# The last tile's second half in two quarters of 256 columns, with a third store at the end

## What is computed

```python
out = conv1d(x, weight, padding=4, groups=4)             # (64, 64, 1024)
y = out + (cond @ c_weight.T)[:, :, None] + bias[None, :, None]
base = y @ kernel + ffn_bias                             # 1024 x 1024
A_eff, B_eff = gate mixed lora_A, lora_B                 # rank 32, one for each of 8 blocks of sequences
delta = (y @ A_eff.T) @ B_eff.T + (y @ A_shared.T) @ B_shared.T
result = x + base + delta
```

## Time and profile before

| | |
|---|---|
| median of 3 runs | 509.15 us (508.51 to 509.65) |
| profiled execution | 507.94 us |
| its span | 506.1 us |
| PE busy | 488.4 us, 96% |
| weight loads (PEld) | 403.1 us, 80% |
| DVE, POOL, ACT busy | 332.9, 272.7, 166.7 us |
| last of PE's products ends | 500.91 us |
| DMA | 65.04 MB, mean 129 GB/s |

### The profile page before, as it was taken

How to read it: one execution, slowest core, us unless ns; L and a number is a source line. 1 busy time by engine, 2 the same in 40 slices (tenths; PEclk the granted TensorE clock), 3 DMA queues, 4 the chain that set the end, 5 groups by cost and what they waited for, 6 DMA issues and landing times.

```text
span 506.1 us, 6740 instructions
## 1 busy us (share of the span) xinstructions
PE 488.4 (96%) x2394; PEld 403.1 (80%) x2394; DVE 332.9 (66%) x384; ACT 166.7 (33%) x210; POOL 272.7 (54%) x157
## 2 busy tenths in 40 slices
PE   2999998999999999999999999999999999999995
PEld 2777886788888888888888888888888888888884
DVE  4786585996938497575939397575948488473411
ACT  2566313341525123331524224331433234331100
POOL 0789943792847439272756529282665619382200
PEclk9999999899999999999999999999999999999998
DMA  8953526751724326241634326241633313241303
GB/s 216 416 217 138 188 69 172 243 199 67 240 94 114 83 70 239 51 128 41 230 102 111 86 52 241 57 124 55 214 117 100 97 29 83 66 122 63 99 27 83
DMA packets 19029, 65.04 MB, mean 129 GB/s; under 512 B 2728, under 2 KB 3368, under 8 KB 18376
## 3 DMA queue, kind: packets, MB, share of 16 engines
q1 hardware_dynamic: 17736, 64.77, 41.3%
q10 hardware_dynamic: 1280, 0.10, 0.2%
HBM read 45.59 MB, written 18.87 MB: 127 GB/s over the span
## 4 chain that ended last, share of the span: by engine, by line
PE 90%; DMA 3%; DVE 2%; POOL 1%; ACT 1%; SPq 1%; issue 0%; ACTq 0%; DVEq 0%
PE main L936 65%; PE rank L949 5%; PE main L941 3%; PE conv L890 3%; PE conv L892 3%; PE conv L891 3%; PE conv L866 2%; DMA cbias<-in_fside_S 2%; PE main L914 1%; PE spare L892 1%; PE spare L891 1%; PE spare L890 1%; SPq L274 1%; DMA b_scratch<-be_lo 1%; PE conv L927 1%; POOL x_lo L360 1%
## 5 line engine op out<-in xcount | busy, mean ns | idle before, releaser
L936 PE MATMUL main<-w_hi,y_hi 128*128 128x512 f32 x512 | 160.1, 391 | 0.0
L936 PE MATMUL main<-w_hi,y_lo 128*128 128x512 f32 x512 | 159.0, 389 | 0.0
L936 PE MATMUL main<-w_lo,y_hi 128*128 128x512 f32 x512 | 158.2, 390 | 0.0
L936 PEld LDWEIGHTS main<-w_lo,y_hi 128*128 128x128 f32 x512 | 96.4, 188 | 20.6
L378 POOL TENSOR_TENSOR y_lo<-y_stage,y_hi 128x512 fp32r<-128x512 f32 x56 | 94.0, 1701 | 34.0 <-ACT y_hi L494 34.0
L936 PEld LDWEIGHTS main<-w_hi,y_lo 128*128 128x128 f32 x512 | 96.1, 188 | 20.3
L936 PEld LDWEIGHTS main<-w_hi,y_hi 128*128 128x128 f32 x512 | 95.3, 188 | 19.4
L358 POOL TENSOR_TENSOR xd_lo<-xd,xd_hi 128x512 fp32r<-128x512 f32 x28 | 39.3, 1404 | 104.2 <-ACT xd_hi L505 104.2
L360 POOL TENSOR_TENSOR x_lo<-x_tr,x_hi 128x1024 fp32r<-128x1024 f32 x28 | 82.6, 2948 | 16.5 <-ACT x_hi L507 16.5
L507 ACT ACTIVATE x_hi<-x_tr 128x1024 fp32r<-128x1024 f32 x28 | 57.7, 2061 | 30.0 <-DVE x_tr L653 30.0
L494 ACT ACTIVATE y_hi<-y_stage 128x512 fp32r<-128x512 f32 x56 | 35.5, 634 | 90.2 <-DVE y_stage L671 90.2
(11 more groups left out here) (105 smaller groups left out, 489.1 us busy)
## 6 DMA issues: line engine op xcount, KB each, us to landing
res<-in_x SPq DMA_DIRECT2D x32, 512.0 KB
out<-res SPq DMA_DIRECT2D x31, 512.0 KB
x_in<-in_x_rows SPq DMA_DIRECT2D x7, 2048.0 KB, 12.8
w_raw<-in_L_ffn_kernel SPq DMA_DIRECT2D x4, 1024.0 KB, 17.8
b_cur<-b_scratch SPq DMA_DIRECT2D x21, 128.0 KB, 3.1
la<-in_L_ffn_lora_A SPq DMA_DIRECT2D x4, 512.0 KB, 8.1
lb<-in_L_ffn_lora_B SPq DMA_DIRECT2D x1, 2048.0 KB, 8.1
x_in<-in_x_rows SPq DMA_DIRECT2D x1, 1048.0 KB, 7.7
```

Source lines behind the costliest of these rows:

```text
L936: mm(main[t][:, n * 512:(n + 1) * 512], lhs, rhs[:, k, n * 512:(n + 1) * 512], start=k == 0 and first, stop=False)
```

## The change

The second half of the last tile is worked as two quarters of 256 columns (q = 2 and 3, columns 512 to 767 and 768 to 1023). Quarter 2 stays in its place in `main[1]`; quarter 3 goes to the first 256 columns of `main[0]`, which tile 30 has left by then (PE waits on `main_free` for that), so that DVE can read quarter 2 while PE writes quarter 3 in another bank. Each quarter has its own 24 products, low-rank product, `tile_done`, DVE add and store.

```diff
+        def last_part(q):
+            return (main[1][:, 512:768], main[0][:, 0:256])[q - 2]
...
-            for h in range(2):
-                sp.wait_ge(main_free, NB * G + h)
-                half = slice(h * 512, (h + 1) * 512)
-                sp.dma_start(out_t[G - 1, (NB - 1) * SB:NB * SB, :, half], res[:, G - 1, half]).then_inc(stored[G - 1], 16)
+            for n, part in enumerate((slice(0, 512), slice(512, 768), slice(768, 1024))):
+                sp.wait_ge(main_free, NB * G + n)
+                sp.dma_start(out_t[G - 1, (NB - 1) * SB:NB * SB, :, part], res[:, G - 1, part]).then_inc(stored[G - 1], 16)
             for g in range(G):
-                sp.wait_ge(stored[g], 16 * (NB + (g == G - 1)))
+                sp.wait_ge(stored[g], 16 * (NB + 2 * (g == G - 1)))
...
-            for h in range(2):
-                half = slice(h * 512, (h + 1) * 512)
-                dve.wait_ge(tile_done, NB * G + h)
-                nc.vector.tensor_tensor(res[:, G - 1, half], main[1][:, half], res[:, G - 1, half],
-                                        ALU.add).then_inc(main_free, 1)
+            dve.wait_ge(tile_done, NB * G)
+            nc.vector.tensor_tensor(res[:, G - 1, 0:512], main[1][:, 0:512], res[:, G - 1, 0:512],
+                                    ALU.add).then_inc(main_free, 1)
+            for q in (2, 3):
+                part = slice(q * 256, (q + 1) * 256)
+                dve.wait_ge(tile_done, NB * G + (q - 1))
+                nc.vector.tensor_tensor(res[:, G - 1, part], last_part(q), res[:, G - 1, part], ALU.add).then_inc(main_free, 1)
...
+            def quarter(q, k):
+
+                yh, yl = y_hi[1][:, 1, k, :], y_lo[1][:, 1, k, :]
+                for lhs, rhs, first in ((yh, w_hi, True), (yh, w_lo, False), (yl, w_hi, False)):
+                    mm(last_part(q), lhs, rhs[:, k, q * 256:(q + 1) * 256], start=k == 0 and first, stop=False)
+
+            def quarter_rank(q):
+                mm(last_part(q), ax_st[0:ROWS, P:2 * P],
+                   b_cur[0:ROWS, :].rearrange("p (oh o8 ol) -> p o8 oh ol", oh=2, o8=R8)[:, 2 * q:2 * q + 2],
+                   start=False, stop=True).then_inc(tile_done, 1)
...
                 if final:
-                    for n in range(2):
-                        for k in range(KC):
-                            dense(h, 1, k, (n,))
-                            if n == 0 and k == 4:
-                                first_rank()
-                        lowrank(1, (n,))
+                    for k in range(KC):
+                        dense(h, 1, k, (0,))
+                        if k == 4:
+                            first_rank()
+                    lowrank(1, (0,))
+                    for k in range(KC):
+                        quarter(2, k)
+                    quarter_rank(2)
+                    pe.wait_ge(main_free, NB * G - 1)
+                    for k in range(KC):
+                        quarter(3, k)
+                    quarter_rank(3)
                     return
```

## The result

The changed kernel takes 506.71 us (median of 11 runs, 505.49 to 507.50), the kernel before, timed beside it in 11 runs, 508.31 (507.77 to 509.67). The ratio is 0.9969, with a 95% interval of 0.9955 to 0.9982: **1.6 us faster, 0.9 to 2.3**. A second timing on another occasion gave 0.9972 (0.9958 to 0.9985), 1.4 us; two of its twelve runs, of 992 and 1728 us, are left out of that ratio. The forecast was 0.8 us and 508.4, with a range down to 507.4; half of the miss in the absolute number is the kernel before, whose first three runs (median 509.15) lay above the median of all eleven.

What follows compares the result with a forecast made beforehand. The end was taken to be bound by PE's matmuls, then the last add and store. Terms +0.27 (PE), -0.27 (DVE), -0.8 (last store) and 0 (queue) gave -0.8 us: 508.4 us, range 507.4 to 509.8.

Steps and rivals of the forecast that it cites:

- The bound: End of the kernel: PE's back-to-back matmuls, then one DVE add and the last store set the end.
- PE +0.27, DVE -0.27: Last half tile: 50 products of 256 columns end 0.27 us later; the halved last add saves 0.27 us.
- The third DMA on SP and the wait before the last quarter: Third quarter's store issue on SP (0.60 us) and PE's wait on main_free: both hidden, no cost.
- The last store -0.8: Last store, 128 KB instead of 256 KB: 0.8 us shorter, bounds none to 1.3 us.
- The engines: DMA stores: 128 data packets, so 8 for each of 16 engines, whatever the row width.
- Rival 3: Last stores: a packet costs the same at 1 KB as at 2 KB; +1.6 us, 510.7 us; chance 0.08.
- The queue, 0: Third quarter's store in the DMA queue: adds 0.9 to 1.0 us, drained as the last store starts; nothing charged.
- Rival 1: Last store: its time is the way to memory and back, not bytes; gain 0 to 0.3, 509.0 us; chance 0.25.
- Rival 2: Last store: whole 2.6 us halves, or third quarter's traffic keeps engines going; -1.3 us, 507.8 us; chance 0.12.
- The number: Whole kernel: 0.8 us off the median of 509.15 us gives 508.4 us.

## Why the prediction was right or wrong

*The bound*: right. The gain lies where the chain said, behind PE's last product, and every tail in the runs adds up from PE, add, issue and wait.

*PE +0.27, DVE -0.27*: right. The products stood 0.120 us apart (0.119 from the convolutions), the border from first to last product's end is 502.08 - 495.92 = 6.16 against 5.84, +0.32; the add takes 0.424 (0.426 worked out). With one store in place of two the kernel was back at 10.55.

*The third DMA on SP and the wait before the last quarter*: hidden, as said. The bank cost nothing where it was changed, and 0.76 us where it was taken away and PE had to wait.

*The last store -0.8*: **this is the step that failed**; it measured -1.4. The line of 0.8 us fixed and 1.8 us per 256 KB was drawn through a store with 4 KB packets and one with 2 KB packets, and I used it at 1 KB as if bytes were its only variable, so that half of the bytes saved 0.9. The runs show no part that stays: the opening, the first 32 packets, fell from 1.07 to 0.39 us, and the rest, with half the bytes, from 1.33 to 0.61, together 0.68 + 0.72 = 1.40. The wait before the first byte (1.23 us before, 1.24 after) and behind the last (0.26 in both) did not change. With the opening as it was, the same sum would have given 0.7. The 128 KB transfers of b_cur, which I took as the nearest row by size (3.1 us), are loads with 4 KB rows, and were no bound for this one.

*The engines*: wrong, though nothing in the sum hangs on it. The packet counts were read as 8 data packets for each of 16 engines, and the account of the kernel before says that the stores are shared out over all 16. The traces fit 8 engines with 16 packets each. Rival 3's price of 2.6 / 8 = 0.32 us a packet is thereby 0.16, and 0.084 in the steady part by the records.

*The queue, 0*: right in size. 128 KB more in line took 7.2 - 6.4 = 0.8 us (0.9 to 1.0 expected), and the last store started 0.4 us after the drain.

*The rivals*. Rival 1 is refuted: 1.4 us for 128 KB. By the Trainium skill, "DMA: Bandwidth & Descriptors", section "Anatomy of one DMA — SWDGE (gpsimd) path", it would have been an estimated 0.30 us; these stores, which SP issues, don't follow that fit. Rival 2 had the number, -1.3, and one of its two reasons, that all of the 2.6 us scale; they did more than that (1.0 us, or 2.4 to 1.0 by the records). Its other reason, warm engines, is refuted by the run without the third quarter's store. Rival 3 is refuted by the lone store of 1 KB rows: 2.5 us, where it said 3.9.

*The number*: counted from 509.15, the median of three runs. With 508.31 of eleven and the measured tail it is 508.31 - 1.35 = 507.0, against 506.71. The range started at 507.4 because its lower end was the whole of 1.3 us from the higher median, less 0.4 for the play of the runs. The tail alone would not have left it: 509.15 - 1.35 = 507.8. What took the result below it is for the most part the base, 0.84 us too high, and a median of three runs, of a kernel whose eleven lie 1.9 us apart, needed more than 0.4.

## What to carry to other kernels

Where a kernel ends in compute, add, store, what counts is how long the last piece takes to come home, and a smaller last piece can be worth more than its share of bytes: look at how long its first packets take and at how many DMA engines it runs on, and measure the store alone by cutting it, which takes one line. Before an experiment is read as "half the bytes", count what else it halves. Splitting the compute to get the smaller piece was paid for here by a shorter add; where PE had to wait for DVE between the pieces, 0.76 us of the gain went. When a change touches the last ten microseconds, compare tails from a common instruction, not spans.

## What the runs showed that was not expected

A store in larger packets is not slower once it runs (189 GB/s at 2 KB, 187 and 193 at 1 KB). It is slower to get going: the first 32 packets of a store that finds the engines idle took 0.39 us at 1 KB and 1.07 us at 2 KB, and a second DMA right behind pays hardly any of it. Why is not settled. In the single DMAs on 8 engines a larger packet always came with more bytes for the DMA, and in the pairs the packet size and the number of DMAs changed together; no run had 256 KB in 1 KB packets in a single DMA. On 4 engines the first 16 packets of 2 KB took 0.69 us, which lies between.

The stores of this kernel seem to run on 8 of the 16 engines, which I had not looked for: 8 small packets with each, and a share of 0.51 to 0.55 in the middle. Whether a store spread over all sixteen would bring the last piece home sooner was not tried.

The same DMA takes 1.43 us to issue from ACT and 0.60 from SP. The first 160 us of the program vary by over a microsecond between executions (1.36 between two profiles of one file); what in them varies was not looked for.
